# An LSTM step on one core: every gate product in one scale, a third copy of h, and plain two-column sums

## The reference, cut to what matters

```python
xW = jnp.einsum('ntd,dk->tnk', x, Wx) + b
def step(carry, xw_t):
    prev_h, prev_c = carry
    a = xw_t + prev_h @ Wh                    # (2, 256) @ (256, 1024)
    i = jax.nn.sigmoid(a[:, :Hdim])
    f = jax.nn.sigmoid(a[:, Hdim:2 * Hdim])
    o = jax.nn.sigmoid(a[:, 2 * Hdim:3 * Hdim])
    g = jnp.tanh(a[:, 3 * Hdim:])
    next_c = f * prev_c + i * g
    next_h = o * jnp.tanh(next_c)
    return ((next_h, next_c), next_h)
```

## Time and profile before

| what | value |
|---|---|
| median of 3 runs | 1886.88 us (1886.73 to 1890.24) |
| the profiled execution, span | 1883.0 us |
| PE busy | 1807.7 us (96%) |
| PEld busy | 1604.6 us (85%) |
| DVE busy | 1543.3 us (82%) |
| ACT busy | 855.4 us (45%) |
| POOL busy | 121.4 us (6%) |
| TensorE clock granted | 1.00 in every stretch looked at |

### The profile page before, as it was taken

One profiled execution on the slowest core, in us unless ns is written; L12 is line 12 of the kernel. 1 busy time (PEld: TensorE's weight loads), 2 busy tenths in 40 slices (PEclk: granted clock), 3 DMA queues, 4 the chain that ended last, 5 costly groups with the idle time before them and its releaser, 6 DMA issues.

```text
span 1883.0 us, 111290 instructions
## 1 busy us (share of the span) xinstructions
PE 1807.7 (96%) x45674; PEld 1604.6 (85%) x45674; DVE 1543.3 (82%) x13293; ACT 855.4 (45%) x5545; POOL 121.4 (6%) x403
## 2 busy tenths in 40 slices
PE   9999999999999999999999999999999999999999
PEld 8888888888888888888888888888888888888888
DVE  7888888888888888888888888888888888888885
ACT  4564444444444444444444444444444444444442
POOL 0000000000000000000000000000000000000000
PEclk9999999999999999999999999999999999999999
DMA  6000000000000000000000000000000000000000
GB/s 250 4 4 4 4 7 4 7 4 4 7 4 7 4 4 7 4 7 3 7 4 4 7 4 6 4 4 7 4 7 4 4 7 4 7 4 6 4 4 8
DMA packets 7440, 20.85 MB, mean 11 GB/s; under 512 B 1168, under 2 KB 5648, under 8 KB 6160
## 3 DMA queue, kind: packets, MB, share of 16 engines
q1 hardware_dynamic: 6640, 13.60, 1.9%
q10 hardware_dynamic: 288, 0.13, 0.0%
HBM read 11.63 MB, written 2.10 MB: 7 GB/s over the span
## 4 chain that ended last, share of the span: by engine, by line
DVE 45%; PE 41%; ACT 9%; issue 5%; DVEq 0%
PE gates L835 16%; DVE gates L660 8%; DVE gates L644 8%; ACT gates L354 7%; PE gates L853 7%; DVE to L674 7%; PE gates L842 6%; DVE addend L656 6%; DVE hh L679 4%; DVE gates L675 3%; DVE gates L670 3%; PE acc_lg L879 2%; PE up_rt L873 2%; PE gates L861 2%; DVE hid_rt L629 2%
## 5 line engine op out<-in xcount | busy, mean ns | idle before, releaser
L853 PE MATMUL gates<-hh,wh_lo 128*128 128x24 f16 x8184 | 783.0, 183 | 0.0
L853 PE MATMUL gates<-hh,wh_hi 128*128 128x24 f16 x8184 | 783.0, 183 | 0.0
L853 PEld LDWEIGHTS gates<-hh,wh_hi 128*128 128x128 f16 x8184 | 549.4, 96 | 0.0
L853 PEld LDWEIGHTS gates<-hh,wh_lo 128*128 128x128 f16 x8184 | 548.3, 95 | 0.0
L354 ACT ACTIVATE gates<-gates 128x4 f32<-128x4 f32 x1024 | 161.8, 158 | 826.1 <-DVE gates L644 825.6
L835 PEld LDWEIGHTS gates<-hh,wh_lo 128*128 128x128 f16 x8184 | 271.6, 96 | 268.6 <-DVE hh L679 266.6
L861 PE MATMUL gates<-hh,wh_small 128*128 128x2 f16 x8184 | 489.1, 164 | 0.2 <-issue 0.2
L835 PE MATMUL gates<-hh,wh_lo 128*128 128x24 f16 x8184 | 380.3, 184 | 70.7 <-DVE hh L679 14.2
L644 DVE TENSOR_TENSOR_SCAN gates<-part_fac,gates 128x8 f32<-128x8 f32 x2048 | 295.3, 179 | 159.9 <-PE gates L842 138.8
L842 PE MATMUL gates<-hh,wh_hi 128*128 128x4 f16 x8184 | 370.0, 171 | 0.0
L861 PEld LDWEIGHTS gates<-hh,wh_small 128*128 128x128 f16 x8184 | 349.5, 96 | 0.3 <-issue 0.3
(11 more groups left out here) (230 smaller groups left out, 2594.4 us busy)
## 6 DMA issues: line engine op xcount, KB each, us to landing
rw_sb<-rw SPq DMA_DIRECT2D x2, 2048.0 KB, 22.1
sw_sb<-sw SPq DMA_DIRECT2D x3, 1024.0 KB, 13.6
x_sb<-xT SPq DMA_DIRECT2D x1, 1920.0 KB, 9.4
outT<-osb SPq DMA_DIRECT2D x15, 128.0 KB, 2.3
wh_sb<-wh SPq DMA_DIRECT2D x2, 512.0 KB, 4.4
wx_sb<-wx SPq DMA_DIRECT2D x1, 1024.0 KB, 6.0
x_sb<-xT SPq DMA_DIRECT2D x1, 128.0 KB, 5.0
eye_sb<-eye ACTq DMA_DIRECT2D x1, 64.0 KB, 4.2
```

The source lines that it names most:

```text
L853: mm(copies(q, m, LOW_COPIES)[:, :, :, 1], part, hh[:, c, half:half + 1, :].broadcast_to([P, LOW_COPIES, B]), start=False, stop=False, ski ...
```

## The change

One scale for all products. DVE makes a third fp16 vector, `h_up` = 4096 `h_hi`. `wh_hi` is multiplied with `h_up` and `h_lo`, `wh_lo` with `h_hi`, and every result is in the same scale. `wh_small` is gone; the seeds (`unit`) are 4096 times larger. F and G still have two columns, added by a `tensor_reduce` over pairs in place of the scan. I and O have one column each, next to one another. Two of O's low products come early in place of one low and one high, and within I and O all low products come first, then those with `h_up`, then those with `h_lo`; the numbers of products and their widths stay (the operand tile of some changes).

```diff
-        hh = sb("hh", [P, KC, 2, B], F16)
-        h_lo, h_hi = hh[:, :, 0, :], hh[:, :, 1, :]
+        hh = sb("hh", [P, KC, 3, B], F16)
+        h_lo, h_up, h_hi = (hh[:, :, j, :] for j in (LOW, UP, HIGH))
...
-            for dst, src, by in ((wh_hi[:, :, 0:D], wh_sb[:, :, 0:D], wh_g), (wh_times_lo[:, :, 0:D], wh_sb[:, :, 0:D], wh_g_lo),
+            for q in WH_ORDER:
+                w = slice(q * D, (q + 1) * D)
+                activation(wh_hi[:, :, w], wh_sb[:, :, w], ACT.Identity, scale=wh_g if q == G else s_wh).then_inc(s_hi, 1)
+                activation(wh_times_lo[:, :, w], wh_sb[:, :, w], ACT.Identity, scale=unit if q == G else s_wh_lo).then_inc(s_hi, 1)
...
             def summed(dst, q):
-                return v.tensor_tensor_scan(dst, part_fac[:].rearrange("p c j -> p (c j)"), parts[q], 0.0, ALU.mult, ALU.add)
+                return v.tensor_reduce(dst, parts[q].rearrange("p (c j) -> p c j", j=PARTS), AX.X, ALU.add)
...
-                v.tensor_copy(parts[O], seeds[:, piece % 2, at, O * HC:I * HC, :].rearrange("p c j -> p (c j)"))
+                v.tensor_copy(o_sum, seeds[:, piece % 2, at, O * HC:I * HC, 1])
...
                 if at == HS - 1:
                     dve.wait_ge(s_staged, tile * PIECES + piece + 2)
-                v.tensor_scalar(c_now[:], cs[:, :, 2], 0.5, None, ALU.mult)
+                dve.wait_ge(s_hhi, n + 2)
+                v.tensor_scalar(h_up, h_hi, LO, None, ALU.mult).then_inc(s_hup, 1)
 
                 dve.wait_ge(s_own, 2 * n + 2)
                 v.scalar_tensor_tensor(h_lo, h_hi, -LO, by_batch(h_now), ALU.mult, ALU.add).then_inc(s_hlo, 1)
 
-                v.tensor_copy(parts[I], seeds[:, piece % 2, at, I * HC:GATES, :].rearrange("p c j -> p (c j)")).then_inc(s_seeded, 1)
+                v.tensor_scalar(c_now[:], cs[:, :, 2], 0.5, None, ALU.mult)
+                v.tensor_copy(i_sum, seeds[:, piece % 2, at, I * HC:GATES, 1]).then_inc(s_seeded, 1)
...
+            def in_one(q, w, half, n, at):
+                for m, c in at:
+                    dst = gates[:, q * BANK:q * BANK + n * APART].rearrange("p (r w) -> p r w", w=APART)[:, :, m * B:(m + 1) * B]
+                    last = mm(dst, block_of(w, q, m, c), hh[:, c, half:half + 1, :].broadcast_to([P, n, B]),
+                              start=False, stop=False, skip_group_check=True)
...
                 pe.wait_ge(s_hhi, n + 1)
                 low(F)
                 low(G)
-                one_column(O, blocks[:EARLY // 2])
-
+                in_one(O, wh_lo, HIGH, LOW_COPIES, blocks[:EARLY])
+
+                pe.wait_ge(s_hup, n)
                 pe.wait_ge(s_hlo, n + 1)
                 high(F, 1).then_inc(s_mul, 1)
                 high(G, HIGH_COPIES).then_inc(s_mul, 1)
                 pe.wait_ge(s_seeded, n)
-                one_column(I, blocks)
-                and_low(I, 1).then_inc(s_mulio, 1)
-                one_column(O, blocks[EARLY // 2:])
-                and_low(O, 1).then_inc(s_mulio, 1)
+                in_one(I, wh_lo, HIGH, LOW_COPIES, blocks)
+                in_one(I, wh_hi, UP, LOW_COPIES, blocks)
+                in_one(I, wh_hi, LOW, 1, blocks).then_inc(s_mulio, 1)
+                in_one(O, wh_lo, HIGH, LOW_COPIES, blocks[EARLY:])
+                in_one(O, wh_hi, UP, LOW_COPIES, blocks)
+                in_one(O, wh_hi, LOW, 1, blocks).then_inc(s_mulio, 1)
```

More of the change, by code:

```diff
@@ L24 @@
 PARTS = 2
+LOW, UP, HIGH = range(3)
 LOW_COPIES, HIGH_COPIES = 12, 7
@@ L116, in cond_resid_kernel @@
         parts = [beside(q, HC * PARTS, 0) for q in range(4)]
-        i_sum, o_sum = (parts[q].rearrange("p (c j) -> p c j", j=PARTS)[:, :, PARTS - 1] for q in (I, O))
+        i_sum, o_sum = (beside(q, HC, 0) for q in (I, O))
         gf_seed = gates.rearrange("p (q n) -> p q n", n=BANK)[:, 0:O, 0:HC * PARTS]
-        g_sum, f_sum = (beside(q, HC * PARTS) for q in (G, F))
+        g_sum, f_sum = (beside(q, HC) for q in (G, F))
         tf = beside(F, HC, BESIDE + 32)
@@ L167, in cond_resid_kernel @@
         tops, s_wh, s_wx, s_xin = scale[:, 0, :], scale[:, 3, 0:1], scale[:, 3, 1:2], scale[:, 3, 2:3]
-        sc = sb("sc", [P, 7])
-        unit, two_unit, to_tanh, half_lo, s_wh_lo, wh_g, wh_g_lo = (sc[:, j:j + 1] for j in range(7))
+        sc = sb("sc", [P, 6])
+        unit, two_unit, to_tanh, half_lo, wh_g, s_wh_lo = (sc[:, j:j + 1] for j in range(6))
         xw_scale = sb("xw_scale", [P, 2])
@@ L483, in _ @@
                 power(stage, slice(0, 1), wh_top)
[L485 to L487 removed]
+            for dst, by in ((wh_g, 2.0), (s_wh_lo, LO), (unit, 2.0 * LO), (two_unit, 4.0 * LO)):
+                v.tensor_scalar(dst, s_wh, by, None, ALU.mult).then_inc(s_scale, 1)
             dve.wait_ge(s_scale, 4)
[L489 removed]
             v.reciprocal(to_tanh, two_unit).then_inc(s_scale, 1)
@@ L531, in _ @@
             dve.wait_ge(s_xwc0, MC + 1)
[L532 to L535, removed]
+            for q in (G, F):
+                v.tensor_scalar(parts[q].rearrange("p (c j) -> p c j", j=PARTS)[:, :, 1], xw[:, q * HC:(q + 1) * HC], unit, None, ALU.mult)
+            v.tensor_scalar(i_sum, xw[:, I * HC:(I + 1) * HC], unit, None, ALU.mult)
+            v.tensor_scalar(o_sum, xw[:, O * HC:(O + 1) * HC], unit, None, ALU.mult).then_inc(s_hhi, 1)
             v.memset(hw0[:], 0.0).then_inc(s_hlo, 1)
@@ L823, in _ @@
             mm = nc.tensor.matmul
+            blocks = [(m, c) for m in range(KC) for c in range(KC)]
             def copies(q, m, n):
@@ L828, in copies, with block_of @@
                 return at[:, :, m * B * PARTS:(m + 1) * B * PARTS].rearrange("p r (b j) -> p r b j", j=PARTS)
+            def block_of(w, q, m, c):
+                return w[:, c, (q * KC + m) * P:(q * KC + m + 1) * P]
             def low(q):
                 n = LOW_COPIES
[L833 to L836, removed]
+                for m, c in blocks:
+                    mm(copies(q, m, n)[:, :, :, 0], block_of(wh_lo, q, m, c), hh[:, c, HIGH:HIGH + 1, :].broadcast_to([P, n, B]),
+                       start=False, stop=False, skip_group_check=True)
@@ L838, in high @@
             def high(q, n):
[L840 to L845, removed]
-                return last
[L848 to L860, removed]
-                        last = mm(copies(q, m, n)[:, :, :, 1], wh_small[:, c, w], hh[:, c, 0:1, :].broadcast_to([P, n, B]),
-                                  start=False, stop=True, skip_group_check=True)
+                for m, c in blocks:
+                    last = mm(copies(q, m, n)[:, :, :, 0:2], block_of(wh_hi, q, m, c),
+                              hh[:, c, LOW:UP + 1, :].rearrange("p (r j) b -> p r b j", r=1).broadcast_to([P, n, B, 2]),
+                              start=False, stop=True, skip_group_check=True)
@@ L1007, in lstm @@
             def lstm(s, tile):
-                blocks = [(m, c) for m in range(KC) for c in range(KC)]
                 n = tile * TS + s
```

47 lines of the change are left out of this document (15 added, 32 removed).

## The result

The changed kernel takes 2021.98 us (median of 4, 2019.43 to 2029.12) against 1886.81 us: ratio 1.0719, 95% interval 1.0705 to 1.0733, so 135 us slower. The forecast was 1977 us, 90 slower; the range ended at 1995. The direction was right, and so were the main mechanism (PE's separate wait for h_lo) and its price. Two losses that the prediction put at nothing were missed: one of TensorE's granted clock, and one from the place of an operand in its tile. The profiled execution of the changed kernel is the slowest of the four (span 2027.1 us), so its span is 144 us above the one before.

The account below looks back on a forecast made before the run. One loop of 1,024 dependent steps bounds the kernel, DVE and PE alternating, no engine full, h_lo on the path. 76.7 + 7.2 + 8.3 - 2.0 + 0.1 = 90.3 us gave 1977 us, 4.8% slower; range 1948 to 1995.

Parts of the forecast that it names:

- The wait for h_lo on PE: Before PE's first high product: h_lo's wait becomes a separate instruction, 0.075 us a step, 76.7 us.
- Every eighth step: On DVE before h_up: h_hi's wait becomes an instruction, h_lo 0.065 us later in 127 steps, 8.3 us.
- c/2 behind h_lo: On DVE: c/2 moved behind h_lo delays I's seed by 0.07 us, but hidden, 0.
- h_up on DVE: In the hole where c/2 sat: h_lo starts 0.007 us later (0.003 to 0.013), 7.2 us.
- The reduce: F's sum on DVE: estimated 160 ns, F's branch 0.02 us shorter, but only 0.002 a step gained, -2 us.
- two branches of one length: Before the scan for c: F's sum, tanh and addend, and I's products, end within about 0.01 us.
- I's branch alone sets the scan: Sign at the scan for c: tanh i starts 0.02 us after the addend's start, no longer with it.
- Products: On PE: same number (30 a step), widths and 0.025 us spacing, adjacent columns in place of every second; 0.
- The reduce is dear: Rival at F's sum: PSUM to PSUM reduce takes 222 ns, 134 us slower, 2021 us; chance 0.05.
- h_up's wait moves out: Rival on PE: h_up's wait becomes the instruction, h_lo's rides; 13.5 us, 1900 us, 0.7% slower; chance 0.09.
- not slower: Rival on PE and DVE: wait instructions cost nothing, h_up fits its hole; 1866 or 1885 us; chance 0.06.

Follow-up runs that it names:

- e3: Kernel before with one already met wait (for h_hi) written ahead of PE's wait for h_lo; 1961.58 us, ratio 1.0406.
- e2: Changed kernel with PE's wait for h_lo ahead of h_up's, and DVE's for h_hi ahead of the staged seeds'; 1939.38 us, 1.0285.
- e10: Changed kernel without PE's h_up wait, DVE's two waits swapped, hh padded to four rows, I and O at every second column; 1891.69 us, 1.0026.
- e8: e2 with the sums of F and G by a scan in place of the reduce; 1951.59 us, 1.0348.
- e5: e2 with the tile of h padded from 3 to 4 rows a chunk; 1913.21 us, 1.0149.
- e9: Kernel before with the products of I and O, and their seeds, at adjacent columns; 1919.98 us, 1.0174.
- e11: Changed kernel with the products of I and O at every second column again; 1988.69 us, 1.0536.
- e1: Changed kernel with PE's wait for h_lo written ahead of its wait for h_up; 1955.11 us, 1.0366.
- e7: e2 without PE's wait for h_up; 1911.05 us, 1.0130.
- e6: e2 with the products of I and O at every second column; 1913.15 us, 1.0141.

## Why the prediction was wrong, by its own steps

- **The wait for h_lo on PE.** Right in place and price: 0.075 a step and 76.7 us forecast, 76.6 us measured alone (e3).
- **Every eighth step.** Right: 8.3 us forecast, 0.076 x 127 = 9.7 in the changed kernel; the swap took 0.075 off each (e2).
- **c/2 behind h_lo.** Put at 0, and 0 in the changed kernel; it came to some 3 us only where the wait was gone (e10).
- **h_up on DVE.** h_lo starts 0.011 later (0.003 to 0.013 was the range); but it takes 155 ns and not 162, so only 0.004 to 0.005 reach PE, some 4 us in place of 7.
- **The reduce.** 174 ns, where I estimated 160 from one of 151. That the gain stays in F's branch was wrong in part: G's sum and ACT's queue pass it on (e8), 5 us in place of 2. The prediction read two branches of one length, F's sum and I's products. It left out the third, G's sum and tanh g, behind which tanh i stands on ACT; so "I's branch alone sets the scan" failed too.
- **Products: "Same number, same widths, same 0.025 spacing ... 0".** This step failed, and twice. In the tile of three rows the second chunk's operand begins 12 bytes on. With it G's four high products last 174, 186, 177 and 186 ns and come 25 to 27 ns apart (e2); with 16 bytes on they all last 174 and come 25 apart, and the step is 0.013 shorter, 13 us (e5). And with adjacent columns 16 products a step take 173 ns by the profile in place of 183, and the granted clock was 0.955 in place of 0.999 (e9). The count was misread as well: a step has 40 products of the LSTM, not 30, in both kernels.
- **The clock.** There was no term for it. The front matter lists a granted clock of 1.00 in each stretch, and the copies and fillers stand in the code; I took the clock as given, counted products and widths, and never asked what the columns that nobody reads are there for. It is 33 of the 45 us that are missing (e11 against the changed kernel). e9 gives 33 too, but that the two agree is chance: its profile has 174 us at the lower level and the changed kernel's 263. The steps are the rest: they cost 102 where I had 90. Added up from the runs, 76.6 for the wait, 9.7 for the eighth steps, 13 for the operand and 4 for h_up, less 5 for the reduce, give about 98. So the steps came near the forecast partly because h_up and the reduce were both cheaper than forecast, against the operand's 13; 4 us have no name.
- **The rivals.** "The reduce is dear" gave 2021 us, the measured time, by a mechanism that is out: the reduce is cheaper than the scan (174 against 179 ns). A time that fits is no proof. "h_up's wait moves out" is out by line 995, "not slower" by e3 and e10. That the wait had been read early, as this rival had it, no record shows: in the changed kernel the instruction of line 995 stands from 0.466 to 0.517 after h_hi, behind h_lo's end at 0.427, and the first high load starts at 0.543.

In this kernel a gap of 0.075 us in every step did nothing to the clock (e3, 0.999), and results in adjacent columns, with no wait added, took it to 0.955 (e9). Whether the gap adds to the loss where the columns are adjacent is not shown: the clock rose a little when it went (e1, 0.949 to 0.961 against 0.935 to 0.948).

## What to carry to other kernels

Where an instruction waits for two semaphores, write the one that comes last in time first: in the cases looked at the later ones of the code became an instruction of their own, worth 0.066 to 0.075 us each time that it is the one waited for. Look for EVENT_SEMAPHORE lines ahead of the path's instructions, and drop a wait that another covers (0.010 us a step in e7). After changing where products write, look at the clock: read the granted clock by stretch, since the busy share did not show it (97.05 of 100 us busy at 0.84, 96.16 at 0.98), and compare the duration of one product by form, not only its count and width. The pitch of a small tile is part of the change too (0.013 us a step in e5).

## What the runs showed of the hardware that was not expected

- A product of 24 columns takes 183 ns into every second column of PSUM and 173 ns into adjacent pairs, at the same 25 ns spacing (the ends are the profile's model). With 16 such products a step the granted clock was 0.997 to 1.00 with the first (before, e3, e6, e10, e11) and 0.935 to 0.986 with the second (the changed kernel, e1, e2, e5, e7, e8, e9).
- With the second chunk's operand of 4 elements (8 bytes) 12 bytes into its tile, the second and fourth product of 28 copied columns, which read it, took 186 ns and the third, which reads the first chunk, 177, at a spacing of 25 to 27 ns (medians of e2). With 16 bytes (e5) or 8 bytes (the kernel before) all four took 174, 25 ns apart.
- With adjacent columns the clock's share varies with small things: 0.950 to 0.986 over e1, e2, e5, e7 and e8, which differ in waits, the tile's pitch and the sum. e8 differs from e2 by 5 ns of a DVE operation and has 0.952 against 0.965. Runs of one kernel scatter by about 0.01 (e2 0.959 to 0.972). What decides there is open.
